# Keys and values of all groups made in a first stage and reloaded from DRAM, against keys and values made group by group inside the loop

## The reference, cut to what matters

```
xn = layernorm(x)                                  # x: 8 x 128 x 512, f32
q  = (xn  @ Wq) -> 8 x 32 heads x 128 x 128        # Wq 512 x 4096
k  = (ctx @ Wk) -> 8 x 8 heads x 128 x 128         # Wk 512 x 1024
v  = (ctx @ Wv) -> 8 x 8 heads x 128 x 128
q, k = rope(q), rope(k)                            # x * cos + rotate_half(x) * sin
scores = q k^T / sqrt(128), masked; attn = softmax(scores)   # 4 query heads share one k, v
x = x + tanh(g_xattn) * ((attn v) -> 8 x 128 x 4096) @ Wo    # Wo 4096 x 512
x = x + tanh(g_ffn) * ((silu(xm @ w1 + b1) * (xm @ w2 + b2)) @ w3 + b3)   # xm = layernorm(x), 512 wide
```

## Time and profile before

| | |
|---|---|
| median of 3 runs | 700.46 us (698.74 to 700.66) |
| span of the profiled execution (first to last instruction) | 698.7 us |
| what lies around that span, by the median | 1.8 us |
| PE busy | 674.9 us, 97% |
| DVE busy | 534.2 us, 76% |
| ACT busy | 330.9 us, 47% |
| POOL busy | 355.3 us, 51% |
| PE's share of the chain that ended last | 89% |
| moved by DMA | 32.49 MB |

### The profile page before, as it was taken

How to read it: one execution, slowest core, us unless ns; L and a number is a source line. 1 busy time by engine, 2 the same in 40 slices (tenths; PEclk the granted TensorE clock), 3 DMA queues, 4 the chain that set the end, 5 groups by cost and what they waited for, 6 DMA issues and landing times.

```text
span 698.7 us, 11562 instructions
## 1 busy us (share of the span) xinstructions
PE 674.9 (97%) x3392; PEld 563.0 (81%) x3392; DVE 534.2 (76%) x878; ACT 330.9 (47%) x917; POOL 355.3 (51%) x298
## 2 busy tenths in 40 slices
PE   5878999999999999999999999999999999989998
PEld 4667888888888888888888888888888888868886
DVE  4987878787878788787878787878787878985433
ACT  3536453455345534553445445443545354875310
POOL 4534864486439544754475546653666446632000
PEclk9988999999999999999999999999999999999999
DMA  9700320031003100201021101210031005000002
GB/s 260 229 8 1 94 59 0 1 90 46 14 0 90 30 30 0 84 21 45 0 60 45 45 0 45 60 45 0 15 90 45 0 0 181 2 1 0 1 31 90
DMA packets 39090, 32.49 MB, mean 47 GB/s; under 512 B 4384, under 2 KB 29984, under 8 KB 39072
## 3 DMA queue, kind: packets, MB, share of 16 engines
q1 hardware_dynamic: 36320, 31.20, 14.9%
q0 software_dynamic: 384, 1.05, 0.5%
q10 hardware_dynamic: 2368, 0.01, 0.2%
HBM read 30.16 MB, written 2.10 MB: 46 GB/s over the span
## 4 chain that ended last, share of the span: by engine, by line
PE 89%; DVE 5%; issue 2%; ACT 1%; POOL 1%; DMA 1%; ACTq 0%; POOLq 0%; DVEq 0%
PE f_bank L323 12%; PE f_bank L325 11%; PE f_bank L324 11%; PE o_bank L323 9%; PE o_bank L325 9%; PE o_bank L324 9%; PE s_banks L433 6%; PE t_bank L329 4%; PE pv_bank L323 3%; PE pv_bank L325 3%; PE pv_bank L324 3%; PE s_banks L434 2%; PE pv_bank L329 1%; PE s_banks L325 1%; PE s_banks L323 1%
## 5 line engine op out<-in xcount | busy, mean ns | idle before, releaser
L686 ACT ACTIVATE prob<-prob,small 128x128 f32<-128x128 f32 x256 | 99.7, 391 | 132.1 <-DVE small L1148 132.1
L323 PE MATMUL o_bank<-wo_hi,o_hi 128*128 128x512 f32 x256 | 105.8, 413 | 0.0
L935 POOL TENSOR_TENSOR q<-t_cos,t_sin 128x512 f32<-128x512 f32 x64 | 82.4, 1289 | 45.8 <-DVE t_sin L1094 45.7
L323 PE MATMUL f_bank<-xT_hi,wq_hi 128*128 128x512 f32 x256 | 103.4, 404 | 0.9 <-ACT cT_hi L659 0.6
L325 PE MATMUL o_bank<-wo_hi,o_lo 128*128 128x512 f32 x256 | 100.4, 392 | 0.0
L325 PE MATMUL f_bank<-xT_hi,wq_lo 128*128 128x512 f32 x256 | 100.2, 391 | 0.0
L324 PE MATMUL f_bank<-xT_lo,wq_hi 128*128 128x512 f32 x256 | 100.0, 391 | 0.0
L324 PE MATMUL o_bank<-wo_lo,o_hi 128*128 128x512 f32 x256 | 100.0, 391 | 0.0
L950 POOL TENSOR_TENSOR prob<-prob,small 128x512 f32<-128x512 f32 x64 | 66.6, 1041 | 65.6 <-DVE small L1152 65.6
L659 ACT ACTIVATE o_hi<-pv_bank 128x512 fp32r<-128x512 f32 x64 | 38.2, 597 | 108.9 <-PE pv_bank L325 108.5
L1094 DVE TENSOR_TENSOR t_sin<-f_bank,rope 64x512 f32<-64x512 f32 x128 | 88.2, 689 | 1.8
(11 more groups left out here) (162 smaller groups left out, 1559.3 us busy)
## 6 DMA issues: line engine op xcount, KB each, us to landing
raw<-in_L_xattn_Wq_dram SPq DMA_DIRECT2D x32, 256.0 KB, 2.9
raw<-in_L_xattn_Wo_dram SPq DMA_DIRECT2D x32, 256.0 KB, 2.6
ctx_raw<-in_ctx_dram SPq DMA_DIRECT2D x8, 256.0 KB, 7.0
raw<-in_L_xattn_Wk_dram SPq DMA_DIRECT2D x8, 256.0 KB
raw<-in_L_xattn_Wv_dram SPq DMA_DIRECT2D x8, 256.0 KB
resid<-in_x_dram SPq DMA_DIRECT2D x8, 256.0 KB, 7.0
out_dram<-resid SPq DMA_DIRECT2D x8, 256.0 KB, 2.0
ffn_raw<-in_L_ffn_w_dram SPq DMA_DIRECT2D x7, 256.0 KB, 5.0
```

The source lines that it names most:

```text
L323: nc.tensor.matmul(dst, st[0], mv_[0], start=start, stop=False)
L686: e = nc.scalar.activation(prob[:, k, h, :], prob[:, k, h, :], ACT.Exp, bias=nmin[k][:, h:h + 1], scale=-1.0, accum_out=psum_row[k][:, h:h ...
L935: nc.gpsimd.tensor_tensor(dst, t_cos[:, ts, :], t_sin[:, ts, :], ALU.add).then_inc(pool_rope, 1)
```

## The change

1. A first stage (`STAGE`) makes all 16 K blocks and all 16 V blocks, and the first five Q blocks. Only Q blocks are left in the pairs: two in pairs 1 to 27, one in pairs 28 and 29.
2. V is made with the tokens as the stationary operand, so it comes out as keys x d, for 4 groups at once. Its 16 sets of transposes go.
3. K and V are stored, split in hi and lo, in two DRAM tensors, and each half of a group is reloaded by SP.
4. RoPE: ACT copies the two halves of the bank, swapped, into `t_sin` (`swap`). DVE then multiplies bank by cos (`rot_cos`, which waits for the swap) and `t_sin` by sin in place (`rot_sin`), 128 partitions in one instruction.
5. `Wo` has two buffers (the second in the place of `cT_hi`), raw slots are 8, and POOL makes both lo parts of q (DVE had made one).
6. The statistics of all eight batches stand together in DVE's list, behind the first V block.

```diff
+STAGE = [("K", 0, 0), ("K", 1, 0), ("V", 0), ("V", 1), ("K", 0, 1), ("V", 2), ("K", 1, 1), ("V", 3),
...
+            def load_v(half, group):
+                for t, part in enumerate((v_hi, v_lo)):
+                    sp.dma_start(f32(part[:, half].rearrange("p b d -> p (b d)")),
+                                 v_dram[bass.ds(group * 256 + (2 * half * KVH + t) * 128, 128), :]).then_inc(v_loaded[half], 16)
...
             with sp.Fori(0, KVH - 1) as G:
-                group_loads(G, False)
-            group_loads(KVH - 1, True)
+                for o in range(8):
+
+                    sp.wait_ge(pool_wlo, 8 + 8 * G + o + 1)
...
+                    sp.dma_start(dst, wq_src(G + 1, o) if o < 4 else wo_src(G + 1, o - 4)).then_inc(raw_loaded[o], 16)
+                for half in range(2):
+
+                    sp.wait_ge(pe_score, 8 * G + 4 * half + 4)
+                    load_k(half, G + 1)
+                    sp.wait_ge(pe_pv, 8 * G + 4 * half + 4)
+                    load_v(half, G + 1)
...
+            def pair(gg, c):
+                first = is_first(gg, c)
+                blocks = q_blocks(gg, c)
+                for e in blocks[:1]:
+                    q_block(gg, e)
+                scores(gg, c, 1)
+                for e in blocks[1:]:
+                    q_block(gg, e)
+                prob_transpose(gg, c, 0)
+                if not first:
+                    out_proj(gg, c - 1, 0)
+                pv(gg, c, 0)
+                prob_transpose(gg, c, 1)
+                if not first:
+                    out_proj(gg, c - 1, 1)
+                pv(gg, c, 1)
+                scores(gg, c + 1, 0)
...
+            def swap(r, ts, fixed):
+
+                act.wait_ge(pe_kq, r + 1)
+                if not (fixed and r < 2):
+                    act.wait_ge(pool_rope, r - 1)
+                nc.scalar.activation(t_sin[64:128, ts, :], f_bank[ts][0:64, :], ACT.Copy)
+                nc.scalar.activation(t_sin[0:64, ts, :], f_bank[ts][64:128, :], ACT.Copy).then_inc(act_swap, 1)
...
+            def v_hi_copy(vi):
+                act.wait_ge(pe_v, vi + 1)
+                if vi >= 2:
+                    act.wait_ge(v_stored[vi % 2], 32 * (vi // 2))
+                else:
+                    act.wait_ge(pe_tile, tile_of("rope", 3) + 1)
...
+            def pair(gg, c):
+                blocks = q_blocks(gg, c)
+                chunks = pair_chunks(gg, c)
+                exps(gg, c, 0)
+                for e in blocks[:1]:
+                    swap_q(gg, e)
+                exps(gg, c, 1)
+                pT_hi_copy(gg, c, 0)
+                for e in blocks[1:]:
+                    swap_q(gg, e)
+                q_hi_copy(gg, c + 1, 0)
+                o_hi_copy(gg, c, 0)
+                pT_hi_copy(gg, c, 1)
+                q_hi_copy(gg, c + 1, 1)
+                for ch in chunks:
+                    split_chunk(*ch)
+                o_hi_copy(gg, c, 1)
```

More of the change, by code:

```diff
@@ new lines, in n_of, with is_first, q_blocks, k_index @@
+        def n_of(gg, c, k):
+            return 16 * gg + 2 * c + k
+        def is_first(gg, c):
+            return isinstance(gg, int) and 8 * gg + c == 0
+        def q_blocks(gg, c):
+            if isinstance(gg, int):
+                p = 8 * gg + c
+                if p == 0:
+                    return list(Q_FIRST)
+                if p >= 25:
+                    return [q - 16 * gg for q in Q_LAST.get(p, [])]
+            return [6 + 2 * c, 7 + 2 * c]
+        def k_index(group, half):
+            return K_ORDER.index((group, half))
@@ L188, in wo_src, with wq_src @@
+        def wq_src(group, h):
+            return Wq[:, bass.ds(group * (GH * D) + h * D, D)].rearrange("(t p) c -> p t c", p=128)
         def wo_src(group, h):
             return Wo[bass.ds(group * (GH * D) + h * D, D), :]
[L191 to L204, removed]
-            if r == 0:
[L206 to L211, removed]
@@ L386, in _ @@
             pe.wait_ge(ident_done, 1)
[L387 to L388 removed]
+            for what, b in TILES_AT[-1]:
+                tile(what, b)
             tiles_done(tile_of("ctx", 3))
[L390 to L397 removed]
@@ L996, in _ @@
-            pair(0, 0)
-            with pool.Fori(0, KVH - 1) as g:
-                for c in range(1, 5):
-                    pair(g, c)
-            pair(KVH - 1, 1)
+            kk = 0
+            for i, blk in enumerate(STAGE):
+                if i and STAGE[i - 1][0] == "K":
+                    k_lo_split(kk)
+                    kk += 1
+                if blk[0] == "K":
+                    add_k(kk)
+                elif blk[0] == "Q":
+                    add_q(0, blk[1])
+                for s in SPLITS_AT.get(i, []):
+                    if s not in V_CHUNKS:
+                        first_chunk(s)
+                if i == 35:
+                    q_lo_split(0, 0, 0)
@@ new lines, in _, with pair @@
+            q_lo_split(0, 0, 1)
+            def pair(gg, c, before):
+                blocks = q_blocks(gg, c)
+                for ch in before:
+                    split_chunk(*ch)
+                norm(gg, c, 0)
+                for e in blocks[:1]:
+                    add_q(gg, e)
+                norm(gg, c, 1)
+                q_lo_split(gg, c + 1, 0)
+                for e in blocks[1:]:
+                    add_q(gg, e)
+                q_lo_split(gg, c + 1, 1)
+            pair(0, 0, [])
@@ L1002, in ffn_tile_lo @@
+            split_chunk(*pair_chunks(0, 0)[0])
+            with pool.Fori(0, 3) as gg:
+                for c in range(1, 9):
+                    pair(gg, c, pair_chunks(gg, c - 1))
+            for c in range(1, 6):
+                pair(3, c, pair_chunks(3, c - 1))
             def ffn_tile_lo(t):
@@ new lines, in pair @@
+            def pair(gg, c):
+                first = is_first(gg, c)
+                blocks = q_blocks(gg, c)
+                for e in blocks[:1]:
+                    cos_q(gg, e)
+                recip(gg, c, 0)
+                mask_scores(gg, c, 1)
+                for e in blocks[:1]:
+                    sin_q(gg, e)
+                for e in blocks[1:2]:
+                    cos_q(gg, e)
+                recip(gg, c, 1)
+                pT_lo_split(gg, c, 0)
+                if not first:
+                    add_out(gg, c - 1, 0)
+                for e in blocks[1:2]:
+                    sin_q(gg, e)
+                for e in blocks[2:]:
+                    cos_q(gg, e)
+                    sin_q(gg, e)
+                o_lo_split(gg, c, 0)
+                pT_lo_split(gg, c, 1)
+                if not first:
+                    add_out(gg, c - 1, 1)
+                o_lo_split(gg, c, 1)
+                mask_scores(gg, c + 1, 0)
```

1022 lines of the change are left out of this document (485 added, 537 removed), and 4 rows, old and new, of the table STAGE.

## The result

| | before | after |
|---|---|---|
| median of the runs beside each other | 700.2 us | 887.3 us (881.0 to 892.0) |
| ratio, 95% interval | | 1.268 (1.261 to 1.274) |
| profiled execution, span | 698.7 us | 890.1 us |
| granted clock, mean | 0.992 | 0.914 |

Predicted were 840 us, with a range of 800 to 872. The direction was right, and the time lies 15 us above the range.

What follows compares the result with a forecast made beforehand. PE's own work bound the loop before; after, one chain through DVE's order would. 137.3 + 21.7 + 508.7 + 29.4 + 33.9 + 107.0 = 838.0 us of span, plus 1.8 gives 840 us; range 800 to 872.

Steps and rivals of the forecast that it cites:

- pair 0: First pair, with three blocks, no output projection and a cold clock: 21.7 us.
- 21 plain pairs, pair 1 among them: Loop pairs of two blocks without a wait for a weight chunk: 18.84 us each.
- chunk wait: Pairs 3, 7, ..., 23: ACT's split of a late-loaded weight chunk holds up `o_hi`, 4.9 us each, 29.4 in all.
- pairs 28 and 29: Loop pairs lacking the second swap and its cos: 17.0 us each, 33.9 together.
- end: From the first scores of pair 30 on, same code and same waits as before: 107.0 us.
- the third rival, the clock: PE's clock falls in each pair, 18 matmuls slow down, 2.0 to 4.1 us per pair: 905 us; chance 8%.
- The stretch from 618: In the trace of before, PE idled 2.2 us yet stayed at full clock; used against a falling clock in pairs.
- the chain: Loop: from one masking of k = 0 to the next through swaps, cos, reciprocals and `pv`, 18.84 us a pair.
- The steps into `pv`: In a pair, from the masking of k = 0 to the start of `pv`: 12.76 us.
- step 11: Pair's last part: `pv` of k = 1 to `o_hi` 0.88 us, `o_lo` 0.63, next masking 0.61.
- the stage: Opening up to the first scores: 137.3 us against 46.39 before, with 11.7 us of waits and 3.8 at its end.
- The first rival: PE stays the bound of the loop, 15.2 us a pair, kernel 700 or 688 us; chance 8%.

Runs made afterwards that it cites:

- the fill run: After, with five useless matmuls put on TensorE ahead of `pv` of k = 0 in every pair but the first: 860.0 us (ratio to before 1.231).
- the run with the later split: After, with the first Wq chunk of the next group but one split one pair later (pairs 4, 8, ...): 858.3 us (ratio to before 1.225).

## Why the prediction fell short, step by step

By its own terms, of the profiled execution (span):

| term | predicted | measured | difference |
|---|---|---|---|
| first scores | 137.3 | 134.7 | -2.6 |
| pair 0 | 21.7 | 22.4 | +0.7 |
| 21 plain pairs, pair 1 among them | 395.6 | 433.2 | +37.6 |
| 6 pairs with a chunk wait | 142.4 | 156.0 | +13.5 |
| pairs 28 and 29 | 33.9 | 36.8 | +2.9 |
| end | 107.0 | 107.0 | 0 |

- **Wrong: the third rival, the clock.** The sum put the clock in the pairs at nothing. The step that failed is "The stretch from 618 speaks against it at this density", which left 8% for a clock that falls in each pair. One idle stretch of 2.21 us, at full clock before and after it, was too little to argue from. In after, 2.46 us a pair bring the clock down, and 1.88 us do so in pair 12 (0.50 from 420 to 422); 1.32 us in the fill run do not, and nor do 2.52 us in pair 9 of the run with the later split. So length alone does not tell, and what does stays open. The price is shown: 1.6 us in a plain pair, and 39.5 us over pairs 1 to 27 in the profiles (589.2 us in after, 549.7 with five fill matmuls), of the 52 us between 838.0 and 890.1 (the medians of the two kernels differ by 27). The rival's range per pair (2.0 to 4.1) was too high as well, since the clock comes back during the output projection. The page that was set against the row, in the Trainium skill (TensorE: Matmul & The Clock Gate, "A second HAM failure mode: psum-queue depth-cycling"), says of another kernel that PE's short idles between groups make the clock go to and fro; the trace agrees, with 0.50 in the stretch from 304 to 306.
- **Right: the chain.** 18.84 was worked out, 18.96 measured once the clock stayed up. The steps into `pv` are 12.89 against 12.76, and that they agree so closely is in part luck. The exponentials (1.68 for 1.56) and the swap (1.23 for 1.10), each twice, and the hi part (0.62 for 0.48) were taken 0.64 too short in all; cos with the reciprocal (0.69 for 0.92, from 294.87 to 295.56, twice) were taken 0.46 too long. The two 64-partition copies start 0.60 apart, so the 1.07 taken for them is 1.20, within its bounds; the other estimate, 1.13, is short too, as the second copy starts only when the first has ended.
- **Mis-sized: the chunk wait.** 4.9 was taken. From `pv` of k = 1 to `o_hi` are 6.6 us on average in the six pairs, where step 11 has 0.88, so `o_hi` comes 5.7 later. The piece that was too small is SP's: from the first load of V to the chunk's issue are 1.41 us (309.27 to 310.68), where two issues of 0.35 were taken. From that issue to the split are 3.6 (3.2 to 4.0) with 3.8 taken for the landing. A pair with the wait takes 5.5 us more than a plain one in after, and 6.1 more with five fill matmuls (25.0 against 18.96).
- **Right in sum: the stage** (-2.6), though not in its parts. The first block starts at 11.5, not 12.5. Of the waits the one ahead of the third K block is 2.72 (3 taken), but the one for the normalised x is 0.69 (4 taken) and the next ahead of a K block 1.44 (2 taken); the waits and the slow clock that the prediction lists add up to 11, where its sum has 11.7. What took more than its term in turn was not looked at. The wait at the end (3.94 for 3.8) and the end of the kernel are right.
- **Short: pairs 28 and 29**, 36.8 for 33.9. In both, PE waits 3.8 us ahead of the transposes of k = 0, and the clock falls there too.
- **The first rival** did not come true: no pair of after came near 15.2. But it named the reciprocal behind cos as the one place that decides, and the run that moves both cos products from there shows 15.64 us a pair, though that kernel stands at 762 for the chunk waits and the stage.
- The range: its upper end, 872, is 6 us above the forecast's own range (866) and left the clock's rival (905) outside. With the clock given its due, 840 + 39.5 = 879.5 is within 8 us of the median, and in the profile most of what is left is the chunk wait: the six pairs take 7.8 us more than their term with five fill matmuls (150.2 for 142.4).

## What to carry to other kernels

Before you move work off an engine that is not the bound, look at who is behind the new hand-over in each engine's written order: here a copy that took 1.2 us stood twice in front of a 0.17 us reciprocal, and cost 3.6 us a pair (18.96 against 15.36). Where a change leaves TensorE waiting in every round, add the slower clock behind that wait to the sum, if what runs there is on the chain; a few matmuls of no use in the gap show in one run whether it counts. And when cover is taken from a loop, reorder the loop in the same change: the same work took 887 us and 697 us.

## What the runs showed of the hardware that I had not expected

- Five useless matmuls a pair made the kernel 27 us faster (887.3 to 860.0), and ten were no better than five.
- The in-place product `t_sin`, both of whose inputs lie in SBUF, takes 0.68 us alone and 1.75 when it starts just behind an instruction of GpSimd (timeline of after, POOL and DVE):

```profile
303.08 1.28 POOL L967 TENSOR_TENSOR q_lo<-q,q_hi 128x512 fp32r<-128x512 f32 x1
303.16 1.75 DVE L1122 TENSOR_TENSOR t_sin<-t_sin,rope 128x512 f32<-128x512 f32 x1
```

It ends 0.55 us after GpSimd's does. In after, 30 of its 80 executions are longer than 0.68 (27 take 1.74 or 1.75, three 1.14 to 1.17); each of the 30 starts during an instruction of GpSimd and ends 0.55 us after it. Of the other 50 only three start during one, in its last 0.21 us, and they take 0.68 to 0.76. Before's form, with an operand in PSUM, has none that is longer, though 71 of its 160 start during one. In the loop it costs nothing: no wait of TensorE ends with one of the long ones. The Trainium skill (SBUF — State Buffer, "Who interferes with whom") says that an instruction of VectorE with two SBUF inputs contends with one of GpSimd that reads SBUF, and that the port pair they share is an exclusive lock; the trace agrees, with 0.55 us left to do when GpSimd's instruction ends.
